# One weighing instruction over both halves of a second block, in the Gelu stage of a conv and mixture-of-experts kernel

## The chip, the cores and the metric

The kernel runs on one core of a Trainium2 chip. The metric is the device time of one execution in microseconds (us), the median over several runs. The engines are called TensorE (PE in the profile, PEld for its weight loads), VectorE (DVE), ScalarE (ACT), GpSimd (POOL) and SyncE (SP), which here only issues DMAs. PSUM is the memory into which TensorE writes; SBUF is the working memory.

## The reference

A two-layer network on 32 images of 14 x 14 positions with 256 channels, all in fp32. The part that the change touches is the last of it, a mixture of small experts with an exact Gelu, computed densely: every token head goes through all experts and the weights of the unchosen ones are zero.

```
def _L1_ffn_ref(x, Wm, bm, expert_emb, W1, b1, W2, b2, Wo, bo):
    ...
    h = x @ Wm + bm
    t = h.reshape(bs * L_ * H, HD)              # 8 heads of 32
    w = jax.nn.softmax(t @ expert_emb, axis=-1)  # 16 experts
    topw, topi = jax.lax.top_k(w, K)             # K = 2
    hmid = jax.nn.gelu(jnp.einsum('td,edi->tei', t, W1) + b1, approximate=False)
    eo = jnp.einsum('tei,eio->teo', hmid, W2) + b2
    sel = jnp.take_along_axis(eo, topi[:, :, None], axis=1)
    comb = (sel * topw[:, :, None]).sum(axis=1)
    out = comb.reshape(bs, L_, d)
    return out @ Wo + bo
```

## The kernel before

Earlier stages (the convolution, the first mixture of experts, the gating) take the first 1,413 us of the profile. The rest is the Gelu stage, the last block of the program.

**Units, groups, slots.** The 6272 tokens with 8 heads each are cut into 49 units of 1024 columns (256 tokens x 4 heads). Each unit meets the 16 experts in 4 groups of 4, so there are 196 groups, numbered g. The program of every engine runs over slots k = 0, 1, 2, ...; in slot k TensorE makes the first products of group k and the second products of group k - 1.

**TensorE in a slot.** Four calls of `first` (L2351), one per expert: x times W1, 128 x 1024 in two matmuls of 512 columns, into one of four pairs of PSUM banks (`psA`, 128 x 1024 fp32 each, `PAIRS_PS = 4`). Then `second` (L2362): for each half b of 512 columns, four matmuls of 32 output rows side by side (each recorded twice, 16 records in all), so that one pair of banks holds the second products of four experts. The last matmul of each half raises the semaphore `put`.

**ScalarE** applies Gelu to each `first` result (L2416, 128x1024, PSUM to SBUF) and raises `gel`.

**VectorE** weighs the second products (`weigh`, L2440): it adds the bias, multiplies by the gate weights `wb`, and writes `gacc` (first group of a unit) or `gsum` (the other three). Each instruction raises `got`. Between weighings VectorE works through the steps of `route` (L1680 to L1703), which makes the gate weights of later images.

**GpSimd** adds `gsum` to `gacc` (L2338, three per unit) and sums the four experts' rows that a DMA has turned (L2325, L2330).

**Extras.** Some slots hold one more small product, placed after the first `first` of the slot: `last` (L2387, the output projection of 256 tokens, read by `finish`, L2457), `route_pe` (L1719, turning gate weights, read by L1727) and `fold` (L2373, at the end only). An extra takes no pair of banks of its own. It is a guest in the pair of the second products of group k - 2, of which it uses the first bank only, and so it waits until the weighing has read that:

```
PAIR_OF[uses] = PAIR_OF[BLOCK_USE[k - 2, 0]] if guest else take("got", uses + 1)
...
def wait_room(eng, use):
    if use in GUEST_OF:
        wait(eng, Q["got"], GUEST_OF[use] + 1)
```

The fourth `first` of slot k takes the same pair (pairs go round in turn, five uses a slot and four pairs), and waits until both halves of group k - 2 are weighed, or until the guest is read where there was one. SyncE loads the gate weights of group k + 2 (L2280) once group k - 1 is weighed.

Of the kernel before, what the change touches and what calls it, by code (L numbers as in the profile page):

```python
# [81 lines left out]
def build(nc, x, c1T, c2T, c3T, invts, lut1, lut2, lut3, bn1, bn2, bn3, routerT, w_moe,  # L82
          se_w1T, se_b1, se_w2T, se_b2, se_wgT, se_bg, wm, bm, emb, w1, b1, w2, b2, wo, bo, out):
    with ExitStack() as ctx:
# [2109 lines left out]
        for k in range(SLOTS):  # L2194
            EXTRAS[k] = [kind for kind, table in (("last", LAST), ("route", ROUTE), ("fold", FOLD)) if k in table]
            for e in range(4):
                if k < NG:
                    FIRST_PAIR[4 * k + e] = take("gel", 4 * k + e + 1)
                for kind in EXTRAS[k] if e == 0 else ():
                    EXTRA_USE[kind, k] = uses  # L2200
                    guest = k - 2 < NG
                    PAIR_OF[uses] = PAIR_OF[BLOCK_USE[k - 2, 0]] if guest else take("got", uses + 1)
                    if guest:
                        GUEST_OF[uses] = BLOCK_USE[k - 2, 0]
                        TAKEN[PAIR_OF[uses]] = ("got", uses + 1)
                    uses += 1
            if 0 < k <= NG:
                pair = take("got", uses + NB)
                for b in range(NB):
                    BLOCK_USE[k - 1, b] = uses  # L2210
                    PAIR_OF[uses] = pair
                    uses += 1

        def bank_pair(use):

            return psA[PAIR_OF[use] % PAIRS_PS]
# [13 lines left out]

        def done_group(g):

            return BLOCK_USE[g, NB - 1] + 1 if g >= 0 else 0

        STORES = []
        for tok, n in PARTS:
# [46 lines left out]
        with nc.Block() as block:  # L2283
# [58 lines left out]
            @block.tensor  # L2342
            def _(eng):
                def first(m):
                    w = m // 16
                    if m % 16 == 0:
                        wait(eng, q_stk[w % 2], (w // 2 + 1) * 64)

                    wait_pair(eng, FIRST_PAIR[m])
                    for b in range(NB):  # L2350
                        mm = eng.matmul(psA[FIRST_PAIR[m] % PAIRS_PS][:, b * BLK:(b + 1) * BLK], w1_r[:, m % 16],  # L2351
                                        x_r[:, w % 2, b * BLK:(b + 1) * BLK], start=True, stop=True)
                    mm.then_inc(Q["mm1"], 1)

                def second(g, b):
                    use = BLOCK_USE[g, b]
                    wait(eng, Q["gel"], 4 * g + 4)

                    if b == 0:
                        wait_room(eng, use)  # L2360
                    for e in range(4):
                        mm = eng.matmul(bank_pair(use)[32 * e:32 * e + 32, b * BLK:(b + 1) * BLK], w2_s[:, g % 4 * 4 + e],  # L2362
                                        hid[:, (4 * g + e) % 8, b * BLK:(b + 1) * BLK], start=True, stop=True,
                                        tile_position=(0, 32 * e))
                    mm.then_inc(Q["put"], 1)

                def fold(w, use):
                    tok, n, head, heads = UNITS[w]

                    wait(eng, Q["acc"], 3 * w + 3)  # L2370
                    wait_room(eng, use)
                    for q in range(heads):
                        mm = eng.matmul(bank_pair(use)[q % 4 * 32:q % 4 * 32 + 32, q // 4 * n:(q // 4 + 1) * n], foldm[:],  # L2373
                                        gacc[:, w % 2, q * n:(q + 1) * n], start=True, stop=True,
                                        tile_position=(0, q % 4 * 32))
                    mm.then_inc(Q["put"], 1)

                def last(c, m_, use):
                    n = PARTS[c][1]

                    if 2 * c < MOVED:
                        wait(eng, Q["comb"], 2 * c + 2)
                    else:
                        wait(eng, Q["got"], EXTRA_USE["fold", 4 * min(2 * c + 1, NU - 1) + 6] + 1)
                    wait_room(eng, use)
                    for h in range(2):
                        mm = eng.matmul(bank_pair(use)[:, 0:n], wo_s[:, h, m_ * 128:(m_ + 1) * 128], comb[:, c % 2, h, 0:n],  # L2387
                                        start=(h == 0), stop=(h == 1))
                    mm.then_inc(Q["put"], 1)

                for k in range(SLOTS):
                    if k == 1:
                        eng.wait_ge(Q["w2"], 16)
                    if k == min(LAST):
                        eng.wait_ge(Q["wo"], 16)
                    for e in range(4):
                        if k < NG:
                            first(4 * k + e)
                        if e == 0 and "fold" in EXTRAS[k]:
                            fold(FOLD[k], EXTRA_USE["fold", k])  # L2400
                        if e == 0 and "last" in EXTRAS[k]:
                            last(*LAST[k], EXTRA_USE["last", k])
                        if e == 0 and "route" in EXTRAS[k]:
                            route_pe(eng, ROUTE[k], EXTRA_USE["route", k])
                    for b in range(NB if 0 < k <= NG else 0):
                        second(k - 1, b)

            @block.scalar
            def _(eng):
# [8 lines left out]

            @block.vector
            def _(eng):  # L2420
                def weigh(g, b):
                    use = BLOCK_USE[g, b]
                    w = g // 4
                    if b == 0:
                        wait(eng, q_wb[g % 3], (g // 3 + 1) * 64)
                    if g % 4 == 0:
                        dst = gacc[:, w % 2, b * BLK:(b + 1) * BLK]

                        if b == 0 and w > 1:
                            if w - 2 < MOVED:  # L2430
                                wait(eng, q_part[w % 2], 16 * sums_of(w - 2))
                            else:
                                wait(eng, Q["put"], EXTRA_USE["fold", 4 * w - 2] + 1)
                    else:
                        a = 3 * w + g % 4 - 1
                        dst = gsum[:, a % 2, b * BLK:(b + 1) * BLK]
                        if b == 0:
                            wait(eng, Q["acc"], a - 1)
                    wait(eng, Q["put"], use + 1)
                    eng.scalar_tensor_tensor(out=dst, in0=bank_pair(use)[:, b * BLK:(b + 1) * BLK], scalar=b2_s[:, g % 4:g % 4 + 1],  # L2440
                                             in1=wb[:, g % 3, b * BLK:(b + 1) * BLK], op0=ALU.add,
                                             op1=ALU.mult).then_inc(Q["got"], 1)

                def combine(w, use):
                    tok, n, head, heads = UNITS[w]
                    wait(eng, Q["put"], use + 1)
                    wait(eng, Q["put"], EXTRA_USE["last", LAST_SLOT[w // 2 - 2]] + 1)
                    dst = comb[:, w // 2 % 2, 0:2, 0:n] if heads == NH else comb[:, w // 2 % 2, w % 2, 0:n]
                    src = bank_pair(use)[:, 0:2 * n].rearrange("p (a c) -> p a c", a=2) if heads == NH else bank_pair(use)[:, 0:n]
                    eng.tensor_copy(dst, src).then_inc(Q["got"], 1)  # L2450

                def finish(c, m_, use):
                    n = PARTS[c][1]
                    wait(eng, Q["put"], use + 1)

                    wait(eng, q_st[m_], stored(c))
                    eng.scalar_tensor_tensor(out=fin[:, m_, 0:n], in0=bank_pair(use)[:, 0:n], scalar=bo_s[:, m_:m_ + 1],  # L2457
                                             in1=tokens(c)[:, m_], op0=ALU.add, op1=ALU.add).then_inc(Q["got"], 1)

                for k in range(SLOTS):  # L2460
                    if "last" in EXTRAS[k]:
                        finish(*LAST[k], EXTRA_USE["last", k])
                    if "route" in EXTRAS[k]:
                        route_copy(eng, ROUTE[k], EXTRA_USE["route", k])
                    if "fold" in EXTRAS[k]:
                        combine(FOLD[k], EXTRA_USE["fold", k])
                    for r, i in STEPS.get(k, ()):
                        route(eng, r, (i,))
                    for b in range(NB if 0 < k <= NG else 0):
                        weigh(k - 1, b)  # L2470


def arrays(i):
# [48 lines left out]
```

## Time and profile before

| | us |
|---|---|
| median of 3 runs | 2260.52 (2258.51 to 2262.49) |
| the profiled execution | 2267.11 |
| its span, first to last instruction | 2265.4 |
| Gelu stage in it | 1413 to 2265 |

The profile is one execution. The times below are counted in us from the start of its span. "Idle before" in a row is time in which the engine did nothing just before these instructions, and the name behind the arrow is what ended most of it. In a timeline, consecutive instructions of one kind are one row with their count.

### The profile page before, as it was taken

To read this page: it belongs to the slowest core of one execution; us is meant where nothing else is said; L and a number is where in the kernel's file an instruction comes from. 1 tells how busy PE (TensorE), PEld (TensorE's weight loads), DVE (VectorE), ACT (ScalarE), POOL (GpSimd) and SP (SyncE) were. 2 spreads that over 40 slices of the span, in tenths; PEclk is the share of its full clock that TensorE was granted. 3 is DMA by queue.
4 is the path that set the end of the run, shared out by engine and by line. 5 is a ranking of instruction groups with operands and counts; after the bars stand their busy time and mean duration, and the time that the engine had idled before them with its cause. 6 is when DMAs were issued, how large, how long until landed. Compare 5 with 4: busy or idle time off the path is not lost. (4 is left out here: it accounts for less than half of the span.)

```text
span 2265.4 us, 35459 instructions
## 1 busy us (share of the span) xinstructions
PE 1995.6 (88%) x12482; PEld 1142.2 (50%) x12483; DVE 1334.5 (59%) x2071; ACT 1278.5 (56%) x1634; POOL 932.6 (41%) x700
## 2 busy tenths in 40 slices
PE   6999789999797777398679986999999999999998
PEld 3444355555453565277546654444444444444444
DVE  5666534455455887222258896567776776666633
ACT  2444322222254433022135543999999999999997
POOL 4333121121000477400178841455555555555554
PEclk7999959999899766699869998999999999999999
DMA  2100031121252443377723434899899899999995
GB/s 58 30 24 21 10 107 60 61 72 46 96 211 67 131 139 110 96 210 207 189 72 99 137 104 126 208 230 229 227 232 230 218 233 235 229 231 232 227 237 133
DMA packets 313681, 329.44 MB, mean 145 GB/s; under 512 B 48678, under 2 KB 288886, under 8 KB 313398
## 3 DMA queue, kind: packets, MB, share of 16 engines
q1 hardware_dynamic: 279542, 281.74, 47.3%
q0 software_dynamic: 12288, 25.72, 3.8%
q10 hardware_dynamic: 21696, 19.93, 2.6%
q8 instruction: 95, 1.56, 0.3%
q14 instruction: 60, 0.49, 0.1%
HBM read 227.87 MB, written 99.37 MB: 144 GB/s over the span
## 5 line engine op out<-in xcount | busy, mean ns | idle before, releaser
L2416 ACT ACTIVATE BIG<-psA,b_s 128x1024 f32<-128x1024 f32 x784 | 801.9, 1133 | 42.1 <-PE psA L2351 38.0
L2338 POOL TENSOR_TENSOR BIG<-BIG 128x1024 f32<-128x1024 f32 x147 | 361.6, 2460 | 262.7 <-DVE BIG L2440 262.6
L2351 PE MATMUL psA<-x_r,w_r 128*128 128x512 f32 x1568 | 451.6, 422 | 10.9 <-DMA x_r<-hs_d 9.4
L2440 DVE SCALAR_TENSOR_TENSOR BIG<-psA,b_s,BIG 128x512 f32<-128x512 f32 x392 | 288.9, 748 | 245.3 <-PE psA L2362 225.8
L2351 PEld LDWEIGHTS psA<-x_r,w_r 128*128 128x128 f32 x1568 | 272.4, 189 | 244.0 <-ACT BIG L2416 135.4
L2362 PE MATMUL psA<-BIG,w_s 128*32 128x512 f32 x3136 | 377.7, 599 | 0.6 <-ACT BIG L2416 0.6
L1783 POOL DMA_INDIRECT gath<-yg_d,SLOT x128 | 140.2, 1095 | 213.3 <-POOLq L1539 175.4
L2362 PEld LDWEIGHTS psA<-BIG,w_s 128*32 128x32 f32 x3136 | 85.8, 109 | 187.8 <-issue 120.8
L719 DVE TENSOR_REDUCE b_nm<-psN 112x32 f32<-112x512 f32 x128 | 83.3, 686 | 151.9 <-PE psN L616 151.5
L1203 POOL DMA_INDIRECT xg_d<-xnb,SLOT x128 | 135.3, 1057 | 80.6 <-DVE SLOT L1318 44.0
L557 POOL CAST b_pat_r<-BIG 72x3584 fp32r<-72x3584 f32 x16 | 50.8, 3173 | 224.2 <-PE psN L616 216.8
L719 DVE TENSOR_REDUCE a_nm<-psN 98x32 f32<-98x512 f32 x128 | 82.3, 685 | 90.2 <-PE psN L607 90.1
L1616 ACT ACTIVATE xv<-ps 128x512 f32<-128x512 f32 x66 | 39.4, 597 | 158.0 <-PE ps L1576 158.0
L1590 PE MATMUL ps<-BIG,xv 128*128 x528 | 126.4, 383 | 2.0 <-ACT xv L1616 1.2
L2325 POOL TENSOR_TENSOR xv<-xv 128x512 f32<-128x512 f32 x46 | 60.6, 1317 | 128.5 <-DMA xv<-part_d 126.1
L775 ACT ACTIVATE b_exs<-ps 128x1568 f32<-128x1568 f32 x32 | 47.3, 1477 | 108.8 <-PE ps L585 108.8
L580 PE MATMUL ps<-BIG,b_wb 72*128 72x392 f32 x256 | 103.3, 551 | 3.4 <-DVE xv L725 3.4
L1590 PEld LDWEIGHTS ps<-BIG,xv 128*128 128x128 f32 x528 | 96.0, 192 | 13.8 <-issue 3.2
L1631 DVE COPY ex<-ps 128x512 f32<-128x512 f32 x33 | 22.8, 692 | 100.1 <-PE ps L1590 96.5
L616 PE MATMUL psN<-b_wb_r,b_pat_r 73*112 73x128 f32 x512 | 72.4, 290 | 9.4 <-POOL b_pat_r L557 9.0
L616 PEld LDWEIGHTS psN<-b_wb_r,b_pat_r 73*112 73x112 f32 x512 | 62.9, 198 | 31.1 <-DVE b_nm L719 13.6
L1576 PE MATMUL ps<-ident,xv 128*128 128x128 f32 x264 | 41.3, 281 | 41.8 <-DMA xv<-xg_d 25.2
(396 smaller groups left out, 3197.3 us busy)
## 6 DMA issues: line engine op xcount, KB each, us to landing
BIG<-wt_d SPq DMA_DIRECT2D x784, 128.0 KB, 4.2
x_r<-hs_d SPq DMA_DIRECT2D x196, 128.0 KB, 3.9
part_d<-BIG SPq DMA_DIRECT2D x46, 512.0 KB, 5.6
xv<-part_d SPq DMA_DIRECT2D x184, 128.0 KB, 3.1
xg_d<-ex SPq DMA_DIRECT2D x64, 264.0 KB, 3.7
xv<-xg_d SPq DMA_DIRECT2D x66, 256.0 KB, 3.2
BIG<-ypad_d SPq DMA_DIRECT2D x140, 120.0 KB
xv<-x SPq DMA_DIRECT2D x64, 196.0 KB, 2.7
```

The source lines that it names most:

```text
L580: eng.matmul(ps4[:, i, 0:CH], w_, src, start=True, stop=False)
L616: mm = eng.matmul(psN[0:SR, bank, g * 128:(g + 1) * 128], pat_r[0:KR, bank * 4 + g, sub * SR:(sub + 1) * SR], wb_r[0:KR, bank * 4 + g], st ...
L719: eng.tensor_reduce(dst, src, AX.X, ALU.max, negate=True).then_inc(S["max"], 1)
L1203: eng.indirect_dma_start(xg_d.ap(), bass.IndirectOffsetOnAxis(ap=SLOT[:, t * NSUB + s, j:j + 1], axis=0), xnb[:, t % XB, s], None).then_in ...
L1590: m = eng.matmul(psZ[:, u, r * C:(r + 1) * C], xt[:, u, r, h * 128:(h + 1) * 128], w_moe_s[:, bass.ds(e * (2 * C) + h * C, C)], start=(h = ...
L1783: eng.indirect_dma_start(gath[:, c % GB, 2 * s + j], None, yg_d.ap(), bass.IndirectOffsetOnAxis(ap=SLOT[:, c * NSUB + s, j:j + 1], axis=0) ...
L2325: eng.tensor_tensor(f[:, 0:2], f[:, 0:2], f[:, 2:4], ALU.add).then_inc(Q["half"], 1)
L2338: eng.tensor_tensor(gacc[:, w % 2], gacc[:, w % 2], gsum[:, a % 2], ALU.add).then_inc(Q["acc"], 1)
L2351: mm = eng.matmul(psA[FIRST_PAIR[m] % PAIRS_PS][:, b * BLK:(b + 1) * BLK], w1_r[:, m % 16], x_r[:, w % 2, b * BLK:(b + 1) * BLK], start=Tr ...
L2362: mm = eng.matmul(bank_pair(use)[32 * e:32 * e + 32, b * BLK:(b + 1) * BLK], w2_s[:, g % 4 * 4 + e], hid[:, (4 * g + e) % 8, b * BLK:(b + ...
L2416: eng.activation(hid[:, m % 8], psA[FIRST_PAIR[m] % PAIRS_PS][:], ACT.Gelu, bias=b1_s[:, m % 16:m % 16 + 1]).then_inc(Q["gel"], 1)
L2440: eng.scalar_tensor_tensor(out=dst, in0=bank_pair(use)[:, b * BLK:(b + 1) * BLK], scalar=b2_s[:, g % 4:g % 4 + 1], in1=wb[:, g % 3, b * BL ...
```

## The change

The two weighing instructions of 128x512 become one of 128x1024, over both banks of the pair. The `put` semaphore is raised once for a pair, by the last of all the matmuls of `second`, and `got` once, by the one weighing. A use number stands now for the whole pair, not for a half, so the guest's wait (`GUEST_OF[use] + 1`) now names the end of the whole weighing.

```
-                    PAIR_OF[uses] = PAIR_OF[BLOCK_USE[k - 2, 0]] if guest else take("got", uses + 1)
+                    PAIR_OF[uses] = PAIR_OF[BLOCK_USE[k - 2]] if guest else take("got", uses + 1)
                     if guest:
-                        GUEST_OF[uses] = BLOCK_USE[k - 2, 0]
+                        GUEST_OF[uses] = BLOCK_USE[k - 2]
...
-                pair = take("got", uses + NB)
-                for b in range(NB):
-                    BLOCK_USE[k - 1, b] = uses
-                    PAIR_OF[uses] = pair
-                    uses += 1
+                BLOCK_USE[k - 1] = uses
+                PAIR_OF[uses] = take("got", uses + 1)
+                uses += 1
...
-                def second(g, b):
+                def second(g):
...
-                    if b == 0:
-                        wait_room(eng, use)
-                    for e in range(4):
-                        mm = eng.matmul(bank_pair(use)[32 * e:32 * e + 32, b * BLK:(b + 1) * BLK], w2_s[:, g % 4 * 4 + e],
+                    wait_room(eng, use)
+                    for b in range(NB):
+                        for e in range(4):
+                            mm = eng.matmul(bank_pair(use)[32 * e:32 * e + 32, b * BLK:(b + 1) * BLK], w2_s[:, g % 4 * 4 + e],
...
                     mm.then_inc(Q["put"], 1)
...
                     wait(eng, Q["put"], use + 1)
-                    eng.scalar_tensor_tensor(out=dst, in0=bank_pair(use)[:, b * BLK:(b + 1) * BLK], scalar=b2_s[:, g % 4:g % 4 + 1],
-                                             in1=wb[:, g % 3, b * BLK:(b + 1) * BLK], op0=ALU.add,
-                                             op1=ALU.mult).then_inc(Q["got"], 1)
+                    eng.scalar_tensor_tensor(out=dst, in0=bank_pair(use)[:], scalar=b2_s[:, g % 4:g % 4 + 1],
+                                             in1=wb[:, g % 3], op0=ALU.add, op1=ALU.mult).then_inc(Q["got"], 1)
```

VectorE's instructions around the first `last` product of the stage, before the change (the last of the three numbers in a line is the tile's shape; L2457 reads the `last` product, L2440 weighs):

```order
L2457 SCALAR_TENSOR_TENSOR BIG<-psA,bo_s,V 128x256
L1680 TENSOR_REDUCE rs<-rt 98x32
L1682 TENSOR_REDUCE rs<-rt 98x32
L2440 SCALAR_TENSOR_TENSOR BIG<-psA,b_s,BIG 128x512 x2
L1727 COPY wts<-psA 128x392
L1684 TENSOR_TENSOR rt<-rt,rs 98x512
L2440 SCALAR_TENSOR_TENSOR BIG<-psA,b_s,BIG 128x512 x2
```

And the same place after it, where the weighing is L2436 and `finish` is L2452:

```order
L2452 SCALAR_TENSOR_TENSOR BIG<-psA,bo_s,V 128x256
L1680 TENSOR_REDUCE rs<-rt 98x32
L1682 TENSOR_REDUCE rs<-rt 98x32
L2436 SCALAR_TENSOR_TENSOR BIG<-psA,b_s,BIG 128x1024
L1727 COPY wts<-psA 128x392
L1684 TENSOR_TENSOR rt<-rt,rs 98x512
L2436 SCALAR_TENSOR_TENSOR BIG<-psA,b_s,BIG 128x1024
```

Nothing else has moved on VectorE: a pair of weighings has become one instruction at the same place. TensorE's order around the same `last` product (L2385 after the change; L2349 `first`, L2360 `second`), after the change:

```order
L2349 MATMUL psA<-x_r,w_r 128x512 x8
L2360 MATMUL psA<-BIG,w_s 32x512 x8
L2349 MATMUL psA<-x_r,w_r 128x512 x2
L2385 MATMUL psA<-xv,wo_s 128x256 x2
L2349 MATMUL psA<-x_r,w_r 128x512 x6
L2360 MATMUL psA<-BIG,w_s 32x512 x8
```

TensorE's order is the same as before, row by row; only what its semaphore waits stand for has changed.

## Rows read from the trace of the kernel before

**Rows 1.** Gelu stage: length, busy us of PE, PEld, DVE, ACT, POOL; granted clock, DMA:

```profile
1420.00:2256.00 836.00, 827.22 (x4952) 394.46 (x4951) 544.58 (x679) 796.53 (x779) 456.77 (x238) 1.00 0.90 224
```

**Rows 2.** Groups of instructions by line and shape, from 1413 us on:

```profile
L2338 POOL TENSOR_TENSOR BIG<-BIG 128x1024 f32<-128x1024 f32 x147 | 361.6, 2460 | 262.7 <-DVE BIG L2440 262.6
L2440 DVE SCALAR_TENSOR_TENSOR BIG<-psA,b_s,BIG 128x512 f32<-128x512 f32 x392 | 288.9, 748 | 245.3 <-PE psA L2362 225.8 <-POOL BIG L2338 14.8 <-DMA BIG<-wt_d 3.0
...
L2387 PEld LDWEIGHTS psA<-xv,wo_s 128*128 128x128 f32 x200 | 37.3, 194 | 10.5 <-issue 1.7 <-DVE BIG L2440 1.1 <-DVE xv L2450 0.8
...
L2457 DVE SCALAR_TENSOR_TENSOR BIG<-psA,bo_s,V 128x256 f32<-128x256 f32 x48 | 23.2, 484 | 34.6 <-PE psA L2387 34.6
...
L1719 PE MATMUL psA<-ident,rt 98*128 98x98 f32 x56 | 7.2, 252 | 5.5 <-DVE BIG L2440 5.5
```

**Rows 3.** Who waited for whom from 1413 us on: us, times, longest:

```profile
DVE BIG L2440 <- PE psA L2362: 225.8, 132, 15.7
...
PE psA L1719 <- DVE BIG L2440: 5.5, 6, 1.9
...
PEld psA L2351 <- DVE BIG L2440: 4.2, 9, 1.4
```

**Rows 4.** Timeline of one slot without an extra: start, us, engine:

```profile
1703.54 1.92 PE L2362 MATMUL psA<-BIG,w_s 128*32 128x512 f32 x16
...
1704.77 1.51 DVE L2440 SCALAR_TENSOR_TENSOR BIG<-psA,b_s,BIG 128x512 f32<-128x512 f32 x2 [1.65 <-PE psA L2362]
...
1706.43 0.77 PEld L2351 LDWEIGHTS psA<-x_r,w_r 128*128 128x128 f32 x4 [0.27 <-ACT BIG L2416]
...
1707.56 1.92 PE L2362 MATMUL psA<-BIG,w_s 128*32 128x512 f32 x16
```

**Rows 5.** Timeline of a slot with a `last` product:

```profile
1711.58 1.92 PE L2362 MATMUL psA<-BIG,w_s 128*32 128x512 f32 x16
...
1712.81 1.51 DVE L2440 SCALAR_TENSOR_TENSOR BIG<-psA,b_s,BIG 128x512 f32<-128x512 f32 x2 [1.92 <-PE psA L2362]
...
1714.00 1.02 PE L2387 MATMUL psA<-xv,wo_s 128*128 128x256 f32 x4
...
1714.68 1.75 PE L2351 MATMUL psA<-x_r,w_r 128*128 128x512 f32 x6
...
1716.35 1.92 PE L2362 MATMUL psA<-BIG,w_s 128*32 128x512 f32 x16
```

**Rows 6.** Timeline of a slot whose weighing came late, with a `last` product:

```profile
1609.86 1.41 DVE L2440 SCALAR_TENSOR_TENSOR BIG<-psA,b_s,BIG 128x512 f32<-128x512 f32 x2 [2.73 <-DMA BIG<-wt_d]
...
1610.75 1.10 PE L2387 MATMUL psA<-xv,wo_s 128*128 128x256 f32 x4 [0.36 <-DVE BIG L2440]
```

**Rows 7.** Timeline: a late weighing and the weights of the fourth `first`:

```profile
1462.18 1.40 DVE L2440 SCALAR_TENSOR_TENSOR BIG<-psA,b_s,BIG 128x512 f32<-128x512 f32 x2
...
1463.63 0.30 PEld L2351 LDWEIGHTS psA<-x_r,w_r 128*128 128x128 f32 x2 [0.30 <-DVE BIG L2440]
```

**Rows 8.** Timeline: `second` of two neighbouring slots, one behind an extra:

```profile
1486.12 1.92 PE L2362 MATMUL psA<-BIG,w_s 128*32 128x512 f32 x16
...
1490.07 1.93 PE L2362 MATMUL psA<-BIG,w_s 128*32 128x512 f32 x16
```

**Rows 9.** Timeline: two stalls of TensorE, and a `second` behind the first:

```profile
1737.53 0.53 PE L1719 MATMUL psA<-ident,rt 98*128 98x98 f32 x4 [1.89 <-DVE BIG L2440]
...
1740.35 2.54 PE L2362 MATMUL psA<-BIG,w_s 128*32 128x512 f32 x16
...
1842.95 0.53 PE L1719 MATMUL psA<-ident,rt 98*128 98x98 f32 x4 [1.13 <-DVE BIG L2440]
```

**Rows 10.** Busy times and granted clock around these two stalls, columns as in rows 1:

```profile
1740.00:1745.00 5.00, 5.00 (x29) 2.06 (x32) 3.83 (x4) 3.22 (x4) 2.00 (x3) 0.83 0.93 233
...
1840.00:1845.00 5.00, 3.87 (x28) 1.91 (x24) 4.17 (x6) 4.07 (x5) 1.85 (x2) 1.00 0.95 261
```

**Rows 11.** DMA issues: the gate weights' loads, with median us to landing:

```profile
BIG<-wt_d SPq DMA_DIRECT2D x784, 128.0 KB, 4.2
```

More of the change, by code:

```diff
@@ L2231, in done_group @@
         def done_group(g):
-            return BLOCK_USE[g, NB - 1] + 1 if g >= 0 else 0
+            return BLOCK_USE[g] + 1 if g >= 0 else 0
         STORES = []
@@ L2353, in first @@
                     mm.then_inc(Q["mm1"], 1)
-                def second(g, b):
-                    use = BLOCK_USE[g, b]
+                def second(g):
+                    use = BLOCK_USE[g]
                     wait(eng, Q["gel"], 4 * g + 4)
-                    if b == 0:
-                        wait_room(eng, use)
-                    for e in range(4):
-                        mm = eng.matmul(bank_pair(use)[32 * e:32 * e + 32, b * BLK:(b + 1) * BLK], w2_s[:, g % 4 * 4 + e],
-                                        hid[:, (4 * g + e) % 8, b * BLK:(b + 1) * BLK], start=True, stop=True,
-                                        tile_position=(0, 32 * e))
+                    wait_room(eng, use)
+                    for b in range(NB):
+                        for e in range(4):
+                            mm = eng.matmul(bank_pair(use)[32 * e:32 * e + 32, b * BLK:(b + 1) * BLK], w2_s[:, g % 4 * 4 + e],
+                                            hid[:, (4 * g + e) % 8, b * BLK:(b + 1) * BLK], start=True, stop=True,
+                                            tile_position=(0, 32 * e))
                     mm.then_inc(Q["put"], 1)
@@ L2404, in _ @@
                             route_pe(eng, ROUTE[k], EXTRA_USE["route", k])
-                    for b in range(NB if 0 < k <= NG else 0):
-                        second(k - 1, b)
+                    if 0 < k <= NG:
+                        second(k - 1)
             @block.scalar
@@ L2420, in _, with weigh @@
             def _(eng):
-                def weigh(g, b):
-                    use = BLOCK_USE[g, b]
+                def weigh(g):
+                    use = BLOCK_USE[g]
                     w = g // 4
-                    if b == 0:
-                        wait(eng, q_wb[g % 3], (g // 3 + 1) * 64)
+                    wait(eng, q_wb[g % 3], (g // 3 + 1) * 64)
                     if g % 4 == 0:
-                        dst = gacc[:, w % 2, b * BLK:(b + 1) * BLK]
-                        if b == 0 and w > 1:
+                        dst = gacc[:, w % 2]
+                        if w > 1:
                             if w - 2 < MOVED:
@@ L2435, in weigh @@
                         a = 3 * w + g % 4 - 1
-                        dst = gsum[:, a % 2, b * BLK:(b + 1) * BLK]
-                        if b == 0:
-                            wait(eng, Q["acc"], a - 1)
+                        dst = gsum[:, a % 2]
+                        wait(eng, Q["acc"], a - 1)
                     wait(eng, Q["put"], use + 1)
-                    eng.scalar_tensor_tensor(out=dst, in0=bank_pair(use)[:, b * BLK:(b + 1) * BLK], scalar=b2_s[:, g % 4:g % 4 + 1],
-                                             in1=wb[:, g % 3, b * BLK:(b + 1) * BLK], op0=ALU.add,
-                                             op1=ALU.mult).then_inc(Q["got"], 1)
+                    eng.scalar_tensor_tensor(out=dst, in0=bank_pair(use)[:], scalar=b2_s[:, g % 4:g % 4 + 1],
+                                             in1=wb[:, g % 3], op0=ALU.add, op1=ALU.mult).then_inc(Q["got"], 1)
                 def combine(w, use):
@@ L2468, in _ @@
                         route(eng, r, (i,))
-                    for b in range(NB if 0 < k <= NG else 0):
-                        weigh(k - 1, b)
+                    if 0 < k <= NG:
+                        weigh(k - 1)
 def arrays(i):
```

## The prediction

> **What bounds the kernel now.** I read the busy times of the Gelu stage first [rows 1]. In 836 us TensorE is busy for 827.22, ScalarE for 796.53 and VectorE for 544.58, and the granted clock is 1.00, the upper level of 2.4 GHz. TensorE stands still for 9 us in all, so nearly every microsecond for which it is made to wait is added to the time. VectorE is idle for a third of the stage; its busy time is no price here. What counts is when the weighing ends, and who waits for that.
>
> So the timeline of one slot comes next. I count from S, the start of the `second` matmuls of group k - 2; behind them come the four `first` of slot k, with the extra after the first of them if there is one. In a plain slot [rows 4] the two weighings run from 1.23 to 2.74 after S (1704.77 to 1706.28, S at 1703.54), so the first half is weighed at 1.98, and the next `second` starts at 4.02. The third `first` is released by ScalarE at 2.89, and the third and fourth fill the time from there to 4.02, so the fourth starts near 3.46. It needs both halves weighed, which they have been since 2.74: 0.7 us to spare. ScalarE paces this slot. Where TensorE paces (behind an extra) a plain slot takes 3.95 [rows 8] and the fourth `first` stands at about 3.39.
>
> In a slot with a `last` product [rows 5] the product starts at 2.42 (1714.00 against 1711.58) and the next `second` at 4.77. The product needs the first half alone. How long TensorE needs from the end of that half is seen where it did wait [rows 6]: the weighing began at 1609.86, its first half ended 0.75 later [rows 2] at 1610.61, the product started at 1610.75, so 0.14. In the usual slot it could have started at 1.98 + 0.14 = 2.12. Only 0.3 us are to spare, and this place is the one that decides.
>
> **The change part by part.**
>
> *The new instruction's length* is in no row. The shapes beside it are: 484 ns for 256 columns of the same operation, 748 for 512 [rows 2], so 264 ns for 256 columns, and 748 + 528 = 1276 for 1024. From below, the columns alone without any fixed part give 1.06 us; from above stand two halves back to back, 1.40 [rows 7], and two whole ones, 1.50. I take 1.28, since the operation is the same and the slope is straight from it.
>
> *Its start.* It waits for the second half's matmuls. Today the second weighing starts at 1.98, right behind the first, so its data are there by then or almost; the first starts at 1.23 with half of the 1.92 us of matmuls done [rows 4], so 0.96 more would be 2.19. I take 2.05. The weighing then runs to 3.33 after S, 0.6 us later than now, though it is shorter by 0.23 than the pair with its wait between.
>
> *The guests' wait.* This is the main term. The extra now waits for the whole weighing: 3.33 + 0.14 = 3.47 in place of 2.42, so TensorE stands for 1.05 us, with the other three `first` and the next `second` queued behind. ScalarE has no store of work to cover that: the one result that it could take is the `first` ahead of the extra. A `last` that had to wait also took 1.10 instead of 1.02 [rows 5, 6], its weights not being loaded ahead: 0.07 more. There are 200/4 = 50 `last` products [rows 2], of which the two at the very end are no guests: 48 x 1.12 = 54 us. There are 56/4 = 14 `route` extras [rows 2]; six of them wait for a late weighing today (5.5 us [rows 3]). Eight cost 1.05 each, 8.4. The six, whose weighing starts late with both halves there, pay only what the whole takes beyond its first half, 1.28 - 0.75 = 0.53 each, 3.2. The folds wait for GpSimd's addition, which starts 0.6 later: two in the stage and the tail, 2. Sum 68.
>
> *The fourth `first`* waits 0.05 behind the weighing (1463.58 to 1463.63 [rows 7]), so until 3.38. That is under the 3.46 of a slot that ScalarE paces, and about level with the 3.39 of the others: 1 us for all. The margin falls from 0.7 to 0.1, though.
>
> *Late weighings.* In 132 of 196 groups VectorE waits for TensorE; in the rest, some 64, `route` steps make it late [rows 3]. It would start those steps 0.6 later, have its own matmuls 0.8 later, and be 0.1 shorter than a back-to-back pair. Nine times a late one holds up a `first` today [rows 3]; there the end moves by 0.6 - 0.1 = 0.5, 4.5 us. Some others lose their margin of 0.1: 1 to 2 us. In slots made longer by a stall VectorE has more room, and loads have more time to land; I take 4 us back for that, most of it from the six late `route` extras.
>
> *Hidden.* 196 instructions fewer on VectorE free about 196 x 0.23 = 45 us there, and nothing waits for it as a whole. GpSimd's additions start 0.6 later, but take 2.46 of a slot of 4 us, with 262.7 us idle before them [rows 2]; only the one behind the last group is on the path. SyncE's loads of gate weights go out 0.6 later; they take 4.2 us to land [rows 11] and are for a group three slots, 12 us, on. Without that cover each would cost up to 0.6.
>
> The sum is 68 + 1 + 6 - 4 = 71, say 70. The profiled execution took 2267.11, so it would come to 2337; that execution lies 6.6 above the median of the runs, 2260.52, to which the same 70 is added: 2330.5.
>
> The Trainium skill has two sentences on this, in "Perfetto Trace Analysis", section "Optimizing Scalar/DVE Operations". Larger operations help if the engine is saturated, since each instruction pays a fixed access time; and where VectorE is not saturated but causes bubbles on other engines, breaking instructions up may let work finish sooner. VectorE's 544.58 of 836 us [rows 1] put this case under the second, which speaks against the change. The first, taken alone, would have it faster. The page's fixed part for PSUM, about 125 ns, saved once in a pair, would make the instruction an estimated 1.37 us and the sum about 80.
>
> **The rivals.**
>
> *The whole costs as much as two halves (1.50).* The fixed part would be paid for each bank. The weighing ends at 3.55: 62 guests pay 0.22 more, 14, and the fourth `first` goes to 3.60, 0.14 to 0.21 over its place in some 130 plain slots, 23. That makes 2330 + 37 = 2367. Against it: ScalarE's and GpSimd's whole-pair instructions run in one piece, and the slope of VectorE's rows.
>
> *ScalarE covers half of the stall.* It is busy for 95% of the stage, and where it paces, it is behind TensorE. Half of the guests' 62 would leave 39: 2300. Against it: a guest slot of 4.77 already shows its whole 0.75 over a plain one.
>
> *The stalls lower TensorE's clock.* Behind a stall of 1.89 us the granted clock fell to the lower level for part of 1740 to 1745 (mean 0.83) and a `second` took 2.54 in place of 1.92; behind one of 1.13 it stayed at 1.00 [rows 9, 10]. The new stalls are of about 1 us, so I don't expect it. If each had such a price, 62 x 0.62 = 38: 2369.
>
> *Faster: late weighings catch up.* A back-to-back pair takes 1.40 [rows 7], the whole 1.28, and VectorE has fewer instructions. If the late weighings no longer held TensorE up, the 5.5 + 4.2 us of [rows 3] would come back: 2251. It decides if the extra reaches its wait after the weighing has ended, that is later than 3.47 after S; it reaches it at 2.42.
>
> *The guests are held up by nothing new,* because something else holds them to 3.47 already: 2260. The 2.42 speaks against it.
>
> **How the numbers follow.** The forecast has 0.76, the 1.50 us weighing 0.06, the clock 0.05, ScalarE's cover 0.07, faster 0.03, no change 0.03. A measurement of this kernel tells about 0.2%, 4.5 us, from no change; so faster 0.03, same 0.03, slower 0.94. Within the forecast the weighing's length moves most: at 1.06 the guests save 62 x 0.22 = 14 and the late ones 2, 2314; at 1.40 the guests pay 7 more and the plain slots, whose margin is 0.1, some 10, 2348. A start at 1.98 or 2.19 moves it by 4 down (62 x 0.07) or some 20 up (62 x 0.14, and the plain slots over their margin). With part of ScalarE's cover below, the range is 2300 to 2354.
>
> **What would show it.** Right: TensorE idle before L2385 (`last`) of about 50 us, released by VectorE's weighing L2436; before L1719 over 10; slots with a `last` of 5.8 to 5.9 us; plain slots of 4.0 as before; the weighing at 1.28 us, 196 times; ScalarE idle for about 110 us; clock 1.00. Wrong: `last` starting at 2.4 after S; a weighing of 1.4 or more, with plain slots of over 4.1; a clock below 1.00 behind the stalls.

## The result and the profile after

The changed kernel takes 2345.81 us (median of 4 runs, 2345.34 to 2347.28), the kernel before 2259.91 beside it (4 runs, 2258.51 to 2262.49): a ratio of 1.039, 95% interval 1.0371 to 1.0408, or 86 us more. The forecast was 2330.5, from 2300 to 2354.

The busy times of the Gelu stage after the change, columns as in [rows 1]:

```profile
1420.00:2336.00 916.00, 851.02 (x4953) 379.38 (x4952) 501.52 (x483) 807.02 (x780) 460.04 (x238) 1.00 0.81 205
```

The stage is 80 us longer than in the profile of before. VectorE works 43 us less (501.52 against 544.58), which bought nothing. TensorE stands still for 65 us in place of 9, at a granted clock of 1.00 as before. The groups by line and shape after the change, to be read against [rows 2]:

```profile
L2414 ACT ACTIVATE BIG<-psA,b_s 128x1024 f32<-128x1024 f32 x784 | 811.7, 1115 | 109.6 <-PE psA L2349 109.0
...
L2436 DVE SCALAR_TENSOR_TENSOR BIG<-psA,b_s,BIG 128x1024 f32<-128x1024 f32 x196 | 251.4, 1283 | 352.2 <-PE psA L2360 349.7 <-POOL BIG L2336 2.3
...
L2385 PE MATMUL psA<-xv,wo_s 128*128 128x256 f32 x192 | 52.9, 398 | 45.4 <-DVE BIG L2436 45.4
...
L1719 PE MATMUL psA<-ident,rt 98*128 98x98 f32 x56 | 7.4, 255 | 13.1 <-DVE BIG L2436 13.1
```

The weighing takes 1283 ns, where the slope of the shorter ones had given 1276. Ahead of `last` (L2385) and `route_pe` (L1719) TensorE now stands for 45.4 and 13.1 us, released by the weighing each time; before, the weights of `last` waited 1.1 and `route_pe` 5.5. ScalarE, which was to cover some of it in one rival, is itself idle for 109.6 us (38.0 before), waiting for `first`.

The slot with a `last` product that answers to the one in [rows 5], the same group g = 69:

```profile
1737.87 1.92 PE L2360 MATMUL psA<-BIG,w_s 128*32 128x512 f32 x16
...
1739.96 1.28 DVE L2436 SCALAR_TENSOR_TENSOR BIG<-psA,b_s,BIG 128x1024 f32<-128x1024 f32 x1 [2.22 <-PE psA L2360]
...
1741.39 1.10 PE L2385 MATMUL psA<-xv,wo_s 128*128 128x256 f32 x4 [0.93 <-DVE BIG L2436]
...
1743.83 1.06 PE L2360 MATMUL psA<-BIG,w_s 128*32 128x512 f32 x8
```

The weighing begins 2.09 after S and ends at 3.37. The product starts at 3.52 (forecast 3.47; 2.42 before), with 0.93 us of idle time ahead of it, and the slot takes 5.96 in place of 4.77. And the plain slot ahead of it, to be read against [rows 4]:

```profile
1733.78 1.92 PE L2360 MATMUL psA<-BIG,w_s 128*32 128x512 f32 x16
...
1735.87 1.28 DVE L2436 SCALAR_TENSOR_TENSOR BIG<-psA,b_s,BIG 128x1024 f32<-128x1024 f32 x1 [0.37 <-PE psA L2360]
...
1737.20 0.30 PEld L2349 LDWEIGHTS psA<-x_r,w_r 128*128 128x128 f32 x2 [0.34 <-DVE BIG L2436]
```

The weights of the fourth `first` now wait for the weighing too: they load at 1737.20, 3.42 after S, and the next `second` follows at 1737.87, so the slot takes 4.09 and is no longer paced by ScalarE. The list of waits shows this as the rule; before it stood there with 4.2 us in 9 waits [rows 3]:

```profile
PEld psA L2349 <- DVE BIG L2436: 50.1, 131, 0.8
...
PE psA L2349 <- DVE BIG L2436: 3.3, 9, 0.4
```

131 is every slot without an extra, and in each it is the fourth `first` that waits. The 50 us are idle time of the weight loads; of TensorE's own time only 3.3 us show as idle, and in the rest its rows have earlier matmuls still running. What these waits cost is therefore read from the length of the slots, below.

### The profile page after: what moved, and what is told of

It is laid out like the page before. It is cut to its first block and busy times, and to the rows that moved or that the text cites. A ratio compares the mean times of both kernels' runs of the same rounds, so it can differ in the third digit from the quotient of the medians.

```text
span 2345.6 us, 35263 instructions
## 1 busy us (share of the span) xinstructions
PE 2028.2 (86%) x12482; PEld 1134.3 (48%) x12483; DVE 1289.4 (55%) x1875; ACT 1288.8 (55%) x1634; POOL 932.4 (40%) x700
## 5 line engine op out<-in xcount | busy, mean ns | idle before, releaser
L2414 ACT ACTIVATE BIG<-psA,b_s 128x1024 f32<-128x1024 f32 x784 | 811.7, 1115 | 109.6 <-PE psA L2349 109.0
L2349 PE MATMUL psA<-x_r,w_r 128*128 128x512 f32 x1568 | 465.1, 425 | 12.8 <-DMA x_r<-hs_d 9.2
L2436 DVE SCALAR_TENSOR_TENSOR BIG<-psA,b_s,BIG 128x1024 f32<-128x1024 f32 x196 | 251.4, 1283 | 352.2 <-PE psA L2360 349.7
L2349 PEld LDWEIGHTS psA<-x_r,w_r 128*128 128x128 f32 x1568 | 264.5, 189 | 267.2 <-ACT BIG L2414 129.0
L2360 PE MATMUL psA<-BIG,w_s 128*32 128x512 f32 x3136 | 377.0, 598 | 0.5 <-ACT BIG L2414 0.4
L2360 PEld LDWEIGHTS psA<-BIG,w_s 128*32 128x32 f32 x3136 | 82.0, 109 | 189.4 <-issue 143.9
L2385 PE MATMUL psA<-xv,wo_s 128*128 128x256 f32 (+1 forms) x200 | 55.0, 400 | 46.0 <-DVE BIG L2436 45.4
```

The source lines that it names most:

```text
L2414: eng.activation(hid[:, m % 8], psA[FIRST_PAIR[m] % PAIRS_PS][:], ACT.Gelu, bias=b1_s[:, m % 16:m % 16 + 1]).then_inc(Q["gel"], 1)
L2436: eng.scalar_tensor_tensor(out=dst, in0=bank_pair(use)[:], scalar=b2_s[:, g % 4:g % 4 + 1], in1=wb[:, g % 3], op0=ALU.add, op1=ALU.mult).t ...
```

## The experiments

Each ran on the chip beside the kernel before. Where slots are averaged below, they are counted from the start of one group's `second` to the next in the trace.

**Guests wait for both halves.** The kernel before, with the new wait of the guests and nothing else:

```
-                        GUEST_OF[uses] = BLOCK_USE[k - 2, 0]
+                        GUEST_OF[uses] = BLOCK_USE[k - 2, NB - 1]
```

> The kernel before with one index changed: an extra waits until both halves of its host pair are weighed, not the first half alone. Weighing stays two instructions. Theory (the guests' wait on the whole weighing is the main cost): the second half ends at 2.74 after S, so the extra starts at 2.88 in place of 2.42; 48 last products x (0.46 + 0.07) = 25, the route extras 3 to 5, so 2290 us (2285 to 2295), with last slots of 5.3 us and plain slots unchanged at 4.02. Rival (ScalarE covers half of such a stall): about 2275. Rival (the single long instruction and what follows from it is the cost, not the guest's wait): 2260.

Measured: 2288.26 us, ratio 1.0146 (1.012 to 1.0173), so 33 us of loss without a long instruction. In the slot of g = 69:

```profile
1716.06 1.92 PE L2362 MATMUL psA<-BIG,w_s 128*32 128x512 f32 x16
1717.29 1.51 DVE L2440 SCALAR_TENSOR_TENSOR BIG<-psA,b_s,BIG 128x512 f32<-128x512 f32 x2 [1.92 <-PE psA L2362]
...
1718.95 1.10 PE L2387 MATMUL psA<-xv,wo_s 128*128 128x256 f32 x4 [0.30 <-DVE BIG L2440]
```

The product starts at 2.89 after S. The 48 `last` slots take 5.29 us in the mean, plain ones that ScalarE paces 4.03. The wait of the guest alone costs about what the arithmetic said (33 us for 28 to 30), and ScalarE covers none of it that can be seen.

**Pairs of their own.** The changed kernel, with the extras no longer guests:

```
-                    guest = k - 2 < NG
+                    guest = False
```

> The changed kernel, with the extras no longer guests: each takes a pair of banks of its own in the rotation, so its wait is on a Gelu long done. The weighing stays one instruction. Theory: the whole cost of the guests goes, 48 x 1.16 + 8 = 64 us, and what stays are the plain slots of 4.09 us and the late weighings (14 us) and the tail, so 2276 to 2284 us, with last slots of 4.8. Rival (the stall is no loss by itself, ScalarE or a load would have held TensorE anyway): over 2310. Rival (a wait takes its place, the third first now waits for the weighing behind an extra): some 2300.

Measured: 2277.94 us, ratio to the kernel before 1.0088 (1.0064 to 1.0112). Of the 86 us, 68 are gone with this one line (1.039 - 1.0088 of 2257). No `last` product waits any more; `last` slots take 4.74 us in the mean, plain ones 4.10 to 4.15, those with a late weighing 4.39, and the wait that is left on the weighing is this:

```profile
PEld psA L2349 <- DVE BIG L2436: 58.5, 146, 0.9
```

Of these waits 131 are, as with the change, the fourth `first` of a slot without an extra. The other 15 are the third `first` behind a `route` or a `fold`, so the second rival above did occur, but in those slots alone. What stays, some 20 us, goes with a `first` behind the whole weighing.

**Pairs of their own, weighing in halves.** The same line in the kernel before:

> The kernel before, with the extras in pairs of their own. Theory: an extra that starts at 2.42 waits for nothing today but in six late route slots, so between 2253 and 2261 us: at best the 5.5 us of those waits come back. Rival (the rotation itself costs): over 2265.

Measured: 2259.48 us, 1.0016 (1.0000 to 1.0032). Giving the extras pairs from the rotation costs nothing that matters by itself, and it gains nothing either. Against the run above, the fused weighing without any guest costs 2277.94 - 2259.48 = 18 us.

**Halves, weighed late.** The kernel before, its first weighing held until the matmuls of both halves are done:

```
-                    wait(eng, Q["put"], use + 1)
+                    wait(eng, Q["put"], BLOCK_USE[g, NB - 1] + 1)
```

> The kernel before with one wait changed: the first of the two weighings waits for the matmuls of both halves, as the single instruction does. The weighings stay two of 512 columns. Theory (what counts is when each half is weighed, not the instruction's length): first half ends at 2.84, second at 3.50 after S; the extras start at 2.97, 55 x (0.55 + 0.07) = 33; the fourth first at 3.55, so plain slots of 4.20, 67 x 0.13 + 47 x 0.26 = 21; late weighings 6 to 8; in all 2315 to 2328 us. Rival (the loss comes from the instruction over two banks): 2260 to 2265.

Measured: 2327.15 us, 1.0307 (1.0278 to 1.0336), with two weighings of 512 columns as before. The slot of g = 68 and what follows it:

```profile
1731.42 1.41 DVE L2440 SCALAR_TENSOR_TENSOR BIG<-psA,b_s,BIG 128x512 f32<-128x512 f32 x2 [0.52 <-PE psA L2362]
...
1732.88 0.30 PEld L2351 LDWEIGHTS psA<-x_r,w_r 128*128 128x128 f32 x2 [0.47 <-DVE BIG L2440]
1733.55 1.92 PE L2362 MATMUL psA<-BIG,w_s 128*32 128x512 f32 x16
...
1736.53 1.10 PE L2387 MATMUL psA<-xv,wo_s 128*128 128x256 f32 x4 [0.40 <-DVE BIG L2440]
```

The pair takes 1.41 from 2.09 on and ends 0.13 later than the whole one; the fourth `first` stands at 3.55 and plain slots take 4.22, 0.12 more than with the whole. The `last` product starts at 2.98, since its half is free earlier, and `last` slots take 5.39 in place of 5.92. The loss follows the ends of the weighings, not the form of the instruction: at the same late start the single instruction is the better one for plain slots, and worse for the guests.

**The extra one place later.** The changed kernel, with the extra behind the second `first` of its slot (the same for `last` and `route`):

```
-                for kind in EXTRAS[k] if e == 0 else ():
+                for kind in EXTRAS[k] if e == 1 else ():
...
-                        if e == 0 and "fold" in EXTRAS[k]:
+                        if e == 1 and "fold" in EXTRAS[k]:
```

> The changed kernel with the extra behind the second first of its slot, not behind the first. It stays a guest that waits for the whole weighing. Theory: TensorE does 0.5 us of useful work in the stall, but the extra still starts at 3.52 after S, and the fourth first, which needs the guest to be read, now waits for that (extra's start + 1.68), so a last slot falls only from 5.95 to about 5.85, and the kernel by some 5 us, to 2338 to 2343. Rival (the stall ahead of the extra is the only thing that counts): 0.5 in each of 62 slots, 31 us, to 2315.

Measured: 2335.89 us, ratio to the kernel before 1.0351 (1.0333 to 1.037), where the changed kernel had 1.039. Half of TensorE's idle time ahead of `last` is gone, 23.6 us for 45.4, and it comes back as a wait that was not there:

```profile
PEld psA L2349 <- DVE BIG L2452: 25.7, 47, 0.5
...
PE psA L2385 <- DVE BIG L2436: 23.6, 48, 1.6
```

The fourth `first` now waits for `finish` (L2452) to read the guest. `last` slots fall from 5.92 to 5.84 only. The time was a little below the range given: 0.0039 of 2256 is 9 us where some 5 were expected; between the two profiles the stage itself differs by 5.

**The kernel before, once more,** for its profile:

> The kernel before, unchanged, for a second profile of it. The profiled execution on which the prediction rests took 2267.1 us where the runs' median is some 2256 to 2260. If that is chance in single stalls, this one has a Gelu stage (first to last second-block matmul) of 828 to 832 us in place of 834.5, with late route slots of under 5 us and no fall of the clock inside the stage; if not, the stage is 834 again.

Measured: 2255.47 us. The rows of the `second` matmuls in the three traces (of before, of this second look, and after the change) give count, min/median/max ns, and the first and last start in us:

```profile
L2362 PE MATMUL psA<-BIG,w_s x3136: 589/592/1062, 1419.9 to 2255.7; 128*32 128x512 f32 x196
```

```profile
L2362 PE MATMUL psA<-BIG,w_s x3136: 588/592/618, 1417.0 to 2244.1; 128*32 128x512 f32 x196
```

```profile
L2360 PE MATMUL psA<-BIG,w_s x3136: 589/592/617, 1420.6 to 2335.3; 128*32 128x512 f32 x196
```

That is 835.8, 827.1 and 914.7 us. The profile on which the prediction rests had 8.7 us in the stage that this one has not. Of these, 6.1 lie in the 14 `route` slots: in the second look one `route` extra waited for the weighing, 1.4 us, not six with 5.5, and the clock didn't fall inside the stage (the slowest matmul took 618 ns, not 1062). VectorE's first `route` step (L1680), which goes ahead of the late weighing, waited for its data for 20.2 us in the first look and for 9.2 in the second:

```profile
DVE rs L1680 <- DMA rt<-ex_d: 20.2, 11, 3.6
```

```profile
DVE rs L1680 <- DMA rt<-ex_d: 9.2, 8, 3.0
```

The second look is even shorter than was expected. Against it, the change costs 87.6 us in the stage, which is what the runs say.

## Why the prediction was right, and where its sizes were off

The time lies within the range, and the mechanism is the one forecast. The sum, term by term. The slots are sorted by what they hold, plain ones by their length in the first profile of before (over or under 3.985 us), and as late where the weighing after the change began more than 2.15 after S. Mean slot in us, and the sum of the difference:

| slots | first look | second look | after | after - first | after - second | forecast |
|---|---|---|---|---|---|---|
| 48 with `last` | 4.77 | 4.75 | 5.92 | 55.5 | 56.4 | 54 |
| 14 with `route` | 4.84 | 4.41 | 5.41 | 7.9 | 14.0 | 11.6 |
| 2 with `fold`, and the tail | 5.24 | 5.15 | 5.91 | 2.0 | 2.2 | 2 |
| 47 plain, TensorE's pace | 3.94 | 3.97 | 4.10 | 7.1 | 6.1 | 1 for both |
| 67 plain, ScalarE's pace | 4.07 | 4.04 | 4.10 | 1.4 | 4.0 | |
| 17 late | 4.06 | 4.06 | 4.39 | 5.6 | 5.6 | 6 |
| given back | | | | | | -4 |

**The guests' wait** was right, in place and in size: 3.52 after S for 3.47, 0.07 more for a product whose weights load after the wait, 48 times. Two runs show that it is the cause of most of the loss: moving this wait alone costs 33 us, and without guests 68 of the 86 us go, while the same line costs the kernel before next to nothing (1.0016).

**The plain slots** were the term that was mis-sized: 8.5 to 10 us where 1 stood. The fourth `first` was to start at 3.38 and did at 3.43. Being under 3.46 was taken to be free, but a `first` that waits also loads its weights late, so the next `second` comes 0.66 behind it, not 0.56. The effect had been counted for `last` and was left out here. The slots that ScalarE paced show it best: their fourth `first` starts no later than before (3.43 in the mean, 3.47 in the second look), and yet they are longer. So the sign "plain slots of 4.0 as before" did not come: they took 4.10. With pairs of their own and no guest, 18 us of loss stay, which this term and the late weighings carry.

**The late weighings** were sized right. The late `route` extras were sized for one execution: against the first look the 14 `route` slots pay 7.9, near the 11.6 less the 4 that were to come back; against the second look, where one was late in place of six, they pay 1.0 each in the mean and nothing comes back. The 70 us, made from the longer execution, were then added to the median of the runs. From execution to execution, 2337 stood against 2347.28, and those 10 us are about what the plain slots cost too much; the rest of the 16 us between forecast and result is the `route` term.

**The weighing's length**, 1.28, was right, and so the rival of 1.50 fell, with its plain slots of over 4.1. **ScalarE's cover** fell: a `last` slot grew by 1.16 us where a stall of 1.12 was forecast, and the guests' wait alone cost 33 us where cover would have left some 15. Its own 109.6 us of idle time prove nothing here, since the same work in a longer stage leaves more of it. **The clock** stayed at 1.00 through 62 stalls of 0.9 us in the mean, the longest 1.6. **Faster** and **no change** fell with the 3.52: the extra reaches its wait long before the weighing has ended, each time.

The two sentences of the Trainium skill ("Perfetto Trace Analysis", section "Optimizing Scalar/DVE Operations") came out so: VectorE was not saturated, and larger instructions saved 43 us of its time for nothing; the other sentence, that smaller instructions may let work finish sooner where bubbles form on other engines, is the one that the runs bear out (2259.48 in halves, 2277.94 whole, without guests). The estimate of 1.37 us took the 125 ns off two profiled rows of 0.75, but the same section of the Trainium skill says that profiled latency is about twice such a figure. By that the estimate is 1.25; 1.283 was measured.

## What to carry to other kernels

Before two instructions are fused, look at what waits for the first of them: a consumer that needs only that part now waits for the end of the whole, and the start moves to the last producer as well. Compare the margin of each consumer with that shift (here 0.3 us and 0.7 us against 1.4 and 0.6); VectorE's own saving of 43 us bought nothing here, because TensorE was the bound. A margin that falls to 0.1 us is not free either: here an operation that waited also loaded its weights late.

## What the runs showed that was not expected

Two executions of the unchanged kernel differed by 8.7 us in a stage of 830, most of it in `route` slots, where VectorE's steps waited for data that landed late; why it landed later in one than in the other is not shown. A sum made against one profiled execution inherits that, and a second look at the kernel before would have shown it. The wait behind a semaphore cost TensorE 0.1 us beyond the wait itself wherever the waiting matmul's weights came after it (0.66 for 0.56 behind the fourth `first`, 1.10 for 1.02 in `last`).
